# Lower expert rows added between the last output tiles, first gathers taken beside the last expert, W_o split later, x loaded first

## The reference

```
x = x + 0.5 * ffn(layernorm(x))     # pass r = 0
x = x + attention(layernorm(x))
x = x + 0.5 * ffn(layernorm(x))     # pass r = 1, same weights
```

## Time and profile before

| what | value |
|---|---|
| median of 3 runs | 2263.69 us (2261.09 to 2263.88) |
| the profiled execution, its own time | 2263.52 us |
| its span | 2261.7 us, 1.8 us less than its time |
| TensorE busy, matmuls | 2030.8 us, 90% |
| VectorE busy | 1283.5 us, 57% |
| ScalarE busy | 1210.9 us, 54% |
| GpSimd busy | 370.1 us, 16% |
| mean granted clock of TensorE | 0.951 of full |

### The profile page before, as it was taken

How to read it: one execution, slowest core, us unless ns; L and a number is a source line. 1 busy time by engine, 2 the same in 40 slices (tenths; PEclk the granted TensorE clock), 3 DMA queues, 4 the chain that set the end, 5 groups by cost and what they waited for, 6 DMA issues and landing times.

```text
span 2261.7 us, 38501 instructions
## 1 busy us (share of the span) xinstructions
PE 2030.8 (90%) x14463; PEld 1751.1 (77%) x14464; DVE 1283.5 (57%) x2528; ACT 1210.9 (54%) x1958; POOL 370.1 (16%) x560
## 2 busy tenths in 40 slices
PE   5399999999995999999999999973999999999990
PEld 2289889898984788878888888852898889897880
DVE  5755554565455648576585765647544554655544
ACT  2267555665463746565565655622655664665530
POOL 0111101110103202112021100101101101111327
PEclk9599999999997999999999999986999999999995
DMA  6113221222122000000000000031122222222215
GB/s 208 61 49 98 89 93 43 85 96 84 53 79 69 20 1 20 9 12 20 1 20 6 15 1 1 1 118 57 58 64 83 66 76 68 71 92 91 74 55 149
DMA packets 84177, 133.15 MB, mean 59 GB/s; under 512 B 10201, under 2 KB 65825, under 8 KB 84065
## 3 DMA queue, kind: packets, MB, share of 16 engines
q1 hardware_dynamic: 69472, 94.67, 12.4%
q0 software_dynamic: 14592, 36.93, 5.9%
HBM read 98.84 MB, written 32.70 MB: 58 GB/s over the span
## 4 chain that ended last, share of the span: by engine, by line
PE 76%; PEld 8%; DVE 5%; ACT 3%; issue 2%; POOL 2%; DMA 1%; PEldq 1%; DVEq 0%; SPq 0%; POOLq 0%
PE bank L597 29%; PE bank L616 12%; PE bank L668 12%; PE bank L761 4%; PEld bank L616 4%; PEld bank L597 3%; PE bank L744 3%; PE bank L694 3%; PE bank L749 3%; PE bank L716 3%; POOL halves L450 2%; PE bank L729 2%; PE bank L546 1%; PE bank L703 1%; PE bank L578 1%
## 5 line engine op out<-in xcount | busy, mean ns | idle before, releaser
L597 PE MATMUL bank<-halves 128*128 128x512 f32 (+2 forms) x3744 | 770.4, 366 | 22.5 <-DVE halves L1200 22.5
L597 PEld LDWEIGHTS bank<-halves 128*128 128x128 f32 x3744 | 649.0, 191 | 128.1 <-issue 24.8
L616 PE MATMUL bank<-halves 128*128 128x256 f32 (+1 forms) x3288 | 403.1, 283 | 3.6 <-issue 3.0
L616 PEld LDWEIGHTS bank<-halves 128*128 128x128 f32 (+1 forms) x3288 | 397.3, 189 | 6.3 <-issue 4.6
L862 ACT ACTIVATE temp<-bank,bias_now 128x512 f32<-128x512 f32 (+1 forms) x312 | 200.3, 642 | 367.8 <-PE bank L597 367.5
L1213 DVE SCALAR_TENSOR_TENSOR temp<-bank,bias_fc,temp 128x512 f32<-128x512 f32 (+1 forms) x312 | 216.1, 693 | 226.2 <-ACT temp L862 222.7
L426 POOL DMA_INDIRECT wide<-normed,spare x160 | 164.7, 1030 | 1053.3 <-PE bank L578 856.9
L668 PE MATMUL bank<-halves 128*128 128x512 f32 x1152 | 285.8, 399 | 3.3 <-DVE halves L1341 2.0
L1220 DVE TENSOR_TENSOR halves<-temp,halves 128x512 fp32r<-128x512 f32 (+1 forms) x312 | 198.2, 635 | 126.6 <-ACT halves L814 123.5
L668 PEld LDWEIGHTS bank<-halves 128*128 128x128 f32 x1152 | 211.9, 189 | 51.3 <-DVE halves L1341 2.4
L814 ACT ACTIVATE halves<-bank 128x512 fp32r<-128x512 f32 (+1 forms) x176 | 90.2, 546 | 238.8 <-PE bank L578 124.4
(11 more groups left out here) (179 smaller groups left out, 2133.6 us busy)
## 6 DMA issues: line engine op xcount, KB each, us to landing
expert_out<-rows SPq DMA_DIRECT2D x144, 128.0 KB, 1.7
wide<-in_L_ffn_w_c_fc SPq DMA_DIRECT2D x16, 1024.0 KB, 5.6
wide<-in_L_ffn_w_gate SPq DMA_DIRECT2D x16, 1024.0 KB, 7.7
wide<-in_L_ffn_w_c_proj SPq DMA_DIRECT2D x16, 1024.0 KB, 5.4
normed<-wide SPq DMA_DIRECT2D x8, 1024.0 KB, 4.9
x<-in_L_attn_x SPq DMA_DIRECT2D x4, 1024.0 KB, 9.7
out_x<-x SPq DMA_DIRECT2D x32, 128.0 KB, 2.4
wide<-normed,spare POOLq DMA_INDIRECT x160, 2.8
```

What stands on the lines that cost most here:

```text
L597: m = pe.matmul(bank[at + b][:, 0:w], a[:, kc, j * P:(j + 1) * P], v[:, kc, 0:w], start=(i == 0), stop=(i == len(ps) - 1))
L616: mm = pe.matmul(bank[4 + t % 2][0:m, 0:C], a[:, j, o:o + m], v[:, j, :], start=(k == 0), stop=(k == len(ps) - 1))
```

## The change

Start: the first quarter of x is issued ahead of the five small loads.

Hand-over: GpSimd gathers the lower rows of tiles 0 to 3 when seven experts are stored and the last expert's first two groups of `up` are done, and the upper rows when all is stored. VectorE adds the four lower rows first, splits W_gate and W_v, does the memsets but two, adds the upper rows with the statistics between them, and takes the deviation from a square root by ScalarE and a reciprocal. W_o's split and the memsets of `state` and `far[1]` (whose space it is) come after the normalising. TensorE turns x without waiting for weights, waits for four splits before the projections, and for the fifth and the memsets before the values; ScalarE waits for the fifth before the values.

Tail: the 32 adds of lower rows move into the last expert, ahead of its output tiles 1 to 9, three or four each.

```diff
@@ -316,6 +316,12 @@
 
         @block.sync
         def _(sp):
+            def load_x(i):
+                n = TILES // 4
+                sp.dma_start(x[:, i * n:(i + 1) * n, :],
+                             x_in[0, i * n * P:(i + 1) * n * P, :].rearrange(tok, p=P)).then_inc(x_loaded[i], 16)
+
+            load_x(0)
             sp.dma_start(router[:], router_w.rearrange("(a p) e -> p a e", p=P)).then_inc(small_loaded, 16)
             sp.dma_start(router_bias[:], router_b.rearrange("(a e) -> a e", a=1).to_broadcast([P, E])).then_inc(small_loaded, 16)
             sp.dma_start(rows[0:E * HJ, 0:P], b_fc.rearrange("e a (j p) -> (e a j) p", p=P)).then_inc(small_loaded, 16)
@@ -323,10 +329,8 @@
             sp.dma_start(rows[0:NPAIR, 2 * P:3 * P], b_gate.rearrange("(j p) -> j p", p=P)).then_inc(small_loaded, 16)
             for b in range(2):
                 sp.sem_inc(y_stored[b], 16)
-            for i in range(4):
-                n = TILES // 4
-                sp.dma_start(x[:, i * n:(i + 1) * n, :],
-                             x_in[0, i * n * P:(i + 1) * n * P, :].rearrange(tok, p=P)).then_inc(x_loaded[i], 16)
+            for i in range(1, 4):
+                load_x(i)
             def stage_fc(r, e):
 
                 wait_past(sp, fc_split, (r * E + e) * 8)
@@ -445,9 +449,9 @@
                         load_rows(e + 1, 0)
                         load_rows(e + 1, 1)
 
-                def gather(into, k, i, landed):
+                def gather(into, k, i, landed, held=ROWS):
                     j = k * TILES + i
-                    pool.indirect_dma_start(into, None, expert_out,
+                    pool.indirect_dma_start(into, None, expert_out[0:held, :],
                                             bass.IndirectOffsetOnAxis(ap=read_slot[:, j:j + 1], axis=0)
                                             ).then_inc(landed, 16)
 
@@ -471,15 +475,22 @@
                     nc.gpsimd.tensor_copy(factors.rearrange("p (n c) -> p n c", n=DH),
                                           now.unsqueeze(1).to_broadcast([P, DH, SUPER + 2])).then_inc(factors_made, 1)
 
-                def gather_pair(i):
+                def gather_pair(i, slots=range(TOPK)):
                     if i >= SUPER:
                         pool.wait_ge(combined, i - SUPER + 1)
-                    for k in range(TOPK):
-                        gather(got4[:, i % SUPER, k, :], k, i, rows_got[i % SUPER])
+                    for k in slots:
+                        gather(got4[:, i % SUPER, k, :], k, i, rows_got[i % SUPER], ROWS if k else ROWS - CAP)
 
                 if r == 0:
+                    wait_stored(E - 1)
+                    pool.wait_ge(up_done, (E - 1) * UNITS + 2 * HJ)
+                    for i in range(SUPER):
+                        gather_pair(i, (0,))
                     wait_stored(E)
-                    for i in range(2 * SUPER):
+                    for i in range(SUPER):
+                        pool.wait_ge(rows_got[i], 16)
+                        gather_pair(i, (1,))
+                    for i in range(SUPER, 2 * SUPER):
                         gather_pair(i)
                     pool.wait_ge(att_cleared, ATT_CLEARS)
                     for s in range(NSUP):
@@ -787,12 +798,13 @@
                         values(s + 1)
                     out_projection(s)
 
-                pe.wait_ge(aw_split, 5)
-                pe.wait_ge(att_cleared, ATT_CLEARS)
                 turn_x(0)
+                pe.wait_ge(aw_split, 4)
                 pe.wait_ge(xa_split, KC)
                 project_z(0, 0)
                 project_qk(0, 0)
+                pe.wait_ge(aw_split, 5)
+                pe.wait_ge(att_cleared, ATT_CLEARS)
                 values(0)
                 for s in range(NSUP):
                     supertile(s, s == NSUP - 1)
@@ -916,7 +928,7 @@
                     nc.scalar.activation(rstd_now, var_now, ACT.Ln).then_inc(log_var4_made, 1)
 
                 def inverse_deviation(s):
-                    act.wait_ge(log_var4_made, s + 1)
+                    act.wait_ge(log_var4_made, s)
                     nc.scalar.activation(rstd_now, rstd_now, ACT.Exp, scale=-0.5).then_inc(rstd4_made, 1)
 
                 def split_x(s):
@@ -991,12 +1003,13 @@
                         decays(s + 1, 0)
                         values(s + 1, range(1, 2 * SUPER))
 
-                log_variance(0)
-                inverse_deviation(0)
+                act.wait_ge(var4_made, 1)
+                nc.scalar.activation(rstd_now, var_now, ACT.Sqrt).then_inc(rstd4_made, 1)
                 split_x(0)
                 gate_exp(0, 0)
                 gate_log(0, 0)
                 decays(0, 0)
+                act.wait_ge(aw_split, 5)
                 values(0)
                 for s in range(NSUP):
                     supertile(s, s == NSUP - 1)
@@ -1201,6 +1214,12 @@
                                         as_f32(xt_hi[buf][:, kc, 0:w]), ALU.subtract)
                 i.then_inc(xt_split, 1)
 
+            def add_lower_rows(tiles):
+                dve.wait_ge(earlier_got, TILES * 16)
+                for i in tiles:
+                    v.scalar_tensor_tensor(x[:, i, :], got[0][:, i, :], weight1[:, i:i + 1], x[:, i, :],
+                                           ALU.mult, ALU.add).then_inc(row1_added, 1)
+
             def expert(r, e, last):
                 u = r * E + e
 
@@ -1246,6 +1265,8 @@
                 low(2 * HJ - 1)
                 dve.wait_ge(bias_loaded, u * 16 + 16)
                 for t in range(4):
+                    if last and r == 1 and t:
+                        add_lower_rows(range((t - 1) * TILES // 9, t * TILES // 9))
                     y_out(t)
                 with dve.If(has_last_group(dve, e)):
                     for unit in range(2 * HJ, UNITS):
@@ -1265,6 +1286,8 @@
                         turned(r, e + 1, 0)
                     if last and r == 0 and t in (6, 8):
                         split_attention((t - 6) // 2)
+                    if last and r == 1 and t > 0:
+                        add_lower_rows(range((t - 1) * TILES // 9, t * TILES // 9))
                     y_out(t)
 
             def add_rows(r, i, got_rows):
@@ -1279,10 +1302,6 @@
                         ins.then_inc(combined, 1)
 
             def combine_last():
-                dve.wait_ge(earlier_got, TILES * 16)
-                for i in range(TILES):
-                    v.scalar_tensor_tensor(x[:, i, :], got[0][:, i, :], weight1[:, i:i + 1], x[:, i, :],
-                                           ALU.mult, ALU.add).then_inc(row1_added, 1)
                 for i in range(TILES):
 
                     dve.wait_ge(rows_got[i], (TILES // SUPER * TOPK + 1 if i < SUPER else 1) * 16)
@@ -1291,19 +1310,25 @@
                                            ALU.mult, ALU.add).then_inc(combined, 1)
 
             def attention():
-                for n in range(2, 5):
-                    split_attention(n)
-                dve.wait_ge(aw_split, 5)
-                v.memset(state, 0.0).then_inc(att_cleared, 1)
+                def add_first(k, b):
+                    dve.wait_ge(rows_got[b], (k + 1) * 16)
+                    if k:
+                        dve.wait_ge(row1_added, b + 1)
+                    v.scalar_tensor_tensor(x[:, b, :], got4[:, b, k, :], (weight1, weight2)[k][:, b:b + 1], x[:, b, :],
+                                           ALU.mult, ALU.add).then_inc((row1_added, combined)[k], 1)
+
+                for b in range(SUPER):
+                    add_first(0, b)
+                split_attention(2)
+                split_attention(3)
+                dve.wait_ge(aw_split, 4)
                 v.memset(carry[:, :, 0:1], 0.0).then_inc(att_cleared, 1)
                 v.memset(bank[7][:, 0:DH * (SUPER + 2)], 0.0).then_inc(att_cleared, 1)
-                for t in far:
-                    v.memset(t[:, :, :, HALF], 0.0).then_inc(att_cleared, 1)
+                v.memset(far[0][:, :, :, HALF], 0.0).then_inc(att_cleared, 1)
                 for h in range(2):
                     v.memset(prob[h], 0.0).then_inc(att_cleared, 1)
                 steps.after(v.memset(limit, LIMIT))
                 steps.after(v.memset(limit.rearrange("p (a n) -> p a n", a=SUPER)[:, :, HALF], 0.0))
-                dve.wait_ge(att_cleared, ATT_CLEARS)
                 lower, upper = slice(0, HALF), slice(HALF, P)
 
                 def combine(s, b):
@@ -1441,12 +1466,19 @@
                         tile_stats(i).then_inc(stats_made, 1)
 
                 for b in range(SUPER):
-                    combine(0, b)
-                for b in range(SUPER):
-                    statistics(0, b)
+                    add_first(1, b)
+                    if b:
+                        statistics(0, b - 1)
+                statistics(0, SUPER - 1)
                 variances(0)
-                refine_deviation(0)
+                dve.wait_ge(rstd4_made, 1)
+                steps.after(v.reciprocal(rstd_now, rstd_now))
```

(5 more changed lines are left out.)

## The result

The changed kernel takes 2247.36 us (median of 6 runs, 2243.04 to 2249.40); the kernel before 2263.78 beside it. The ratio is 0.9926, 95% interval 0.9915 to 0.9937: 16.4 us or 0.74% faster. The profiled execution took 2247.8 us, span 2246.1, which is 15.6 under the span of before. The forecast was 2245.5, range 2242 to 2250.5.

The account below looks back on a forecast made before the run. TensorE with its weight loads, 84% of the chain, was untouched; the change targeted three places where TensorE has nothing to do. Savings 9.45 + 8.1 + 0.5 = 18.05 us from 2263.52 gave 2245.5 us, range 2242 to 2250.5.

Parts of the forecast that it names:

- The tail: Behind the last output tile: with the adds moved, the first gather takes 0.95 us instead of 10.40, 9.45 us saved.
- The rival by the lock per instruction: Tail: a gather waits for one add only, the 10.40 us has another cause; time 2255.0 us, chance 0.06.
- a VectorE instruction with two SBUF inputs: Tail and hand-over: such an instruction holds up a gather GpSimd is issuing; an unbroken run lets none in.
- The hand-over: First feed-forward pass to attention: steps summing to 8.1 us saved, bounds 5.2 and 9.5.
- last eviction to the last upper add: Hand-over: four early lower-row gathers let the fourth remaining gather land at 713.2 instead of 718.75, 5.55 us saved.
- last add's start to the variance: Hand-over: one add and two statistics instead of a pair of adds and four statistics, 1.15 us saved.
- variance to normalising: Hand-over: deviation by square root and reciprocal, 0.5 us instead of 2.63, 2.1 us saved.
- normalising to dense matmuls (W_o's split): Hand-over: W_o's split and memsets, 3.0 us placed before the split of x, make it late by 0.3 us.
- the clock's rise later: Hand-over: TensorE's rise from the 1.2 GHz level comes later after its restart, 0.4 us lost.
- The rival that gives this gain back: Hand-over: the freed 8 us are lost to held gathers and TensorE staying at 1.2 GHz; about 2253 us, chance 0.06.
- The start: First 10 us: x's first quarter issued ahead of five small loads brings first statistics to 9.3 us, 0.5 us gained.
- I take 7.0, just behind the quarter: Start: assumed landing time of the small loads, 7.0 us, giving first statistics at 9.3 instead of 9.79.

Follow-up runs that it names:

- e2: The kernel before with only the 32 lower-row adds moved between the last output tiles: 2254.76 us, ratio 0.9963.
- e5: The kernel before with a semaphore wait after each of the 32 lower-row adds behind the last tile: 2257.24 us in one run.
- e6: The kernel before with the 32 lower-row adds replaced by back-to-back instructions reading one SBUF tensor, x left out: 2260.20 us in one run.
- e7: The changed kernel with VectorE's first statistics and deviation ahead of its wait for the small loads and the bias copies: 2241.91 us, ratio 0.9909.
- e11: The kernel of e7 with W_o's split, the state's memset and the wait moved behind the split of x: 2244.73 us, ratio 0.9909.
- e9: The changed kernel with W_o split right behind W_v again, the state's memset staying late: 2247.32 us in one run.
- e8: The changed kernel with the first deviation by logarithm, exponential and refinement again: 2249.92 us in one run.
- e3: The changed kernel with the old start and the old tail, so only the hand-over is new: 2253.92 us, ratio 0.9962.
- e10: The changed kernel without early gathers, the eight first gathers in pairs behind the last store again: 2252.07 us in one run.
- e4: The changed kernel without its new start, the small loads first again: 2244.43 us, ratio 0.9919.

## Why the prediction was right, and where it was not

**The tail was right in mechanism and size.** Forecast 9.45 us, and the first gather went from 10.40 to 0.94. The tail as a whole is 10.1 us shorter between the two profiles, but that is the largest difference that the profiles have: with the held gather of 10.40 us it is 59.2 to 60.0 us in three of them, with the moved adds 49.9 to 51.4 in nine, on average 9.0 less. e2's time was 8.7 less. The moved adds cost nothing: cover and sizes were as worked out (1.66 us for four, forecast 1.6 to 2.0). The rival by the lock per instruction falls with e5. What failed is half a sentence: "a VectorE instruction with two SBUF inputs". One input can do it too (e6), though it need not (the normalising).

**The hand-over was right, 1 us too small.** Forecast 8.1, measured 9.2. By its steps, after minus before between the same events:

| step | forecast | measured |
|---|---|---|
| last eviction to the last upper add | 5.55 | 17.55 - 11.71 = 5.84 |
| last add's start to the variance | 1.15 | 2.36 - 1.18 = 1.18 |
| variance to normalising | 2.1 | 4.06 - 1.86 = 2.20 |
| normalising to dense matmuls (W_o's split) | -0.3 | 5.68 - 5.73 = -0.05 |
| the clock's rise later | -0.4 | 0 |

The mis-sized terms are three. In the first step I costed the four lower adds at 0.50 us each, and they took 1.66 us in all, so that the fourth gather starts 8.8 us behind the last eviction and not 9.2. For the clock I took 0.4 us against a row that said 3.5 us after the dense matmuls, and it was 3.5 again. W_o's split costs 0.15 to 0.2 and not 0.3: from normalising to dense matmuls are 5.73 us in e7 with it, 5.56 in e11 and 5.58 in e9 without. The rest is the normalising, 1.38 us where it took 1.59 before. I had not foreseen that, and its cause stays open: in e8 it takes 1.59 with the same split behind it, in e11 1.43 without. The rival that gives this gain back falls with e3.

**The start was wrong in sign.** The step that failed is "I take 7.0, just behind the quarter". The small loads landed between 7.8 and 8.3 us in the eight profiles with x first, 1.1 to 1.6 us behind the quarter (6.6 and 6.7 in e11 and e7, where VectorE waits for it), so in the six of them that keep the old order of waits VectorE was ready at 10.2 to 10.6 and not at 9.3: 0.4 to 0.9 lost where 0.5 was to be gained. The bounds (5.5 and 9) held. The five small loads are issued while the quarter moves, and the second quarter is issued behind them at 4.41. "DMA: Bandwidth & Descriptors" of the Trainium skill, on queues and rings, has descriptors consumed in ring order on each DMA engine, and the traces agree in that the small loads come behind the quarter (7.8 to 8.3 us against 6.6 to 6.7); how much of the extra 1.1 to 1.6 us is their own latency or the second quarter beside them was not tried.

**The sum.** Forecast 18.05; the parts measured in place give 9.2 + 9.0 - 0.4 = 17.8. That the two are so near is in part luck: the hand-over was forecast 1.1 too small, the tail 0.45 and the start 0.9 too large. The first six runs gave 16.4, all eleven 16.8 against the same kernel of before. For the 1 to 1.4 us between, the profile of the first run has a place: the first eight experts, 3.0 us longer than before, where the change touches nothing. That term was not in my list at all: I had the clock only at the restart. What stays open is whether the changed start makes such a fall more likely. Of the eight profiles with x first six had it (not e7 and e10), of the six with the old order three (e2, e4, e5). That is too few to tell it from chance.

## What to carry to other kernels

When a gather issued by GpSimd takes many microseconds, look at what VectorE does over it: here a run of elementwise instructions from SBUF to SBUF with no wait between them, one every 0.26 or 0.40 us, locked it out until 0.8 us after the run's end. Memsets and a run of four normalising instructions did not, so look for that 0.8 us in the trace. A semaphore wait after each instruction was enough to let the gather in, and work that fits in idle slots earlier is better still. A load that is moved ahead can only bring its engine forward if that engine isn't also waiting for what the load was moved past; move the waits along with the issue.

## What was not expected of the hardware

- Single-input instructions held a gather as two-input ones did, until 0.82 us behind the run: 6.14 us (e6). Four other single-input instructions in a row did not: 0.95 us (the normalising, before). With a wait after each add, 32 adds cost 16.74 us instead of 12.74 and the gathers beside them 0.95 to 1.07 us (e5).
- Small loads of 4 to 32 KB issued behind 1 MB on the same queue landed 1.1 to 1.6 us after it, in the changed kernel 4.3 us after the issue of the last one at 3.69; issued first, they had landed 1.7 us after the issue of the last one at 3.06.
- Two programs that are the same up to that point, with the same pause of TensorE at 305 us, are granted the full 2.4 GHz level after it in one case (e3) and the 1.2 GHz level for some microseconds in the other (e4); over all profiles the stage takes 1.5 to 4 us more with such a fall.
